# One signal for a group's value products, a power as the seed of the inverse roots, and an earlier copy of turned rows

## The chip, the cores and the metric

The kernel runs on one core of a Trainium2 chip. The metric is the device time of one execution in microseconds (us). The core has a matrix engine (TensorE, in the profile PE, with its weight loads as PEld), a vector engine (DVE), an activation engine (ACT), GpSimd (POOL) and an engine that only issues transfers (SP). Each runs its own program in its own order; they meet through semaphores.

## The reference

Four sequences of 1024 tokens, 128 channels, float32:

```
x = u + lru(layernorm(u))                 # linear recurrence, complex diagonal
z = layernorm(x)
h = z + attention(rmsnorm(z) * ln1)       # 16 heads of 8 channels, full softmax
h = h + moe(rmsnorm(h) * ln2)             # 8 experts, two per token
out = x + h

rmsnorm(v) = v * rsqrt(mean(v * v) + 1e-5)
moe: logits = v @ gate.T; the two largest are chosen and weighted by their softmax
     expert e: (silu(v @ w1[e].T) * (v @ w3[e].T)) @ w2[e].T
```

## The kernel before

The kernel has three stages. In the first (to about 245 us) the four sequences go through the recurrence and the projections to queries, keys and values. The second is attention (to about 985 us): 16 quads (a sequence and four of its heads), each with 16 groups g. In a group TensorE makes four column scores (`score_cols`, L1322), each of which ACT turns into `prob` with an exp (L853), two steps of row scores (`score_rows`, L1273) whose maxima DVE takes (L1084), and the value products of the group before (`weigh_values`, L1332): four heads, each on its own 32 columns of the array, into one bank, with two matmul instructions per head in the trace. `prob` is a ring of eight. An exp waits for its score (`col_full`) and for the value product that read its slot before (`pv_done`, set ahead by eight). After groups 7 and 15 the bank is full, ACT copies it to `oT` (`save_o`, L841), and TensorE turns it for DVE.

Behind attention, the tokens go through the routing in eight blocks of 512. Per block, ACT copies the turned attention (`turn_a`), TensorE projects it (`project`), and GpSimd does the rest: `sum_h` adds, squares and sums (L544 to L551) and makes `var` (L553); `norm_h` refines the inverse root by Newton rounds (L561 to L565) and scales the rows to `h_nrm` (L566); TensorE turns them (`turn_h`, L1356) and makes the logits; `pick_two` and `place_tokens` choose two experts per token and give each its slot, with counts from TensorE (`prefix` and `totals`, or `ranks`); `scatter` writes the rows to `by_expert_rows` with eight indirect DMAs. The seed of the root is made on DVE, with integer operations on the bits (`seed`, L1133 and L1136), between `f_mean` and `f_seed`. Blocks 0 to 5 ("early") do this during attention, in quads "even" and "odd", one block for two quads. Blocks 6 and 7 ("late") do it in the expert stage, at tiles given by the table `LATE` on TensorE and ACT and `LATE_SEED` on DVE. Before tile 0, `make_table` lists the 56 tiles of region A (blocks 0 to 5); behind block 7, it lists the 24 tiles of region B (L666 is its last operation).

The expert stage runs over 80 tiles j of 128 rows in 20 groups of four. SP loads a group of x three groups ahead (L401), TensorE turns it in tile 4g+2 (`turn_x`, L1487) and ACT copies it, scaled, to `x_T` (`save_x`, L899), in tile 4g+3. A tile is `up` (L1498) on TensorE, `gate` (L906) on ACT, the product and a copy (L1190, L1198) on DVE, a turning (L1508), `down` (L1518) two tiles later, `save_y` (L914) on ACT, and a write to `by_expert_rows` from SP (L411). Tiles 0 to 55 are region A. When all of A is written, GpSimd fetches each token's two results (`fetch`, L734, 32 tiles of tokens, two indirect DMAs each), and DVE adds them to `xacc` (`combine`, L1203 and L1206), from tile 60 on between its other work. The last eight token tiles wait for region B. The store of `out` follows.

Of the kernel before, what the change touches and what calls it, by code (L numbers as in the profile page):

```python
# [14 lines left out]
P = 128  # L15
# [47 lines left out]
def build_program(nc, x, nu2, theta2, gamma_row, b_pack, b_swap, c_re_t, c_im_t, d_t, ln1, ln2,  # L63
# [3 lines left out]
    with ctx:  # L67
        def sb(name, shape, dt=F32):
            return ctx.enter_context(nc.sbuf_tensor(name, shape, dt))

        def sem(name):
            return ctx.enter_context(nc.semaphore(name))
# [75 lines left out]
        hot = sb("hot", [P, 4, NE])  # L148
        gap = sb("gap", [P, 4])
        weigh = sb("weigh", [P, 2, 4])  # L150
        tanh = sb("tanh", [P, 4])
        slot_f = sb("slot_f", [P, 2, 4])
        slots = sb("slots", [P, 2, 4], I32)
# [43 lines left out]
        zeros, zero_out = sem("zeros"), sem("zero_out")  # L197
        gp_self = sem("gp_self")
        att_st, h_read = sem("att_st"), sem("h_read")
        f_mean, f_seed, f_norm, f_gap, f_hot, f_tanh = (  # L200
            sem(n) for n in ("f_mean", "f_seed", "f_norm", "f_gap", "f_hot", "f_tanh"))
        scattered, f_tab = sem("scattered"), sem("f_tab")
        x_loaded = [sem("x_loaded%d" % r) for r in range(3)]
        y_out = [sem("y_out%d" % r) for r in range(3)]
# [79 lines left out]
        def row_banks(pos):  # L284
            return 2 * (pos % 2)
# [7 lines left out]
        LATE = {2: ("turn_a", 6), 5: ("project", 6), 14: ("turn_h", 6), 17: ("logits", 6), 18: ("turn_a", 7),  # L293
                22: ("ranks", 6), 23: ("project", 7), 33: ("turn_h", 7), 36: ("logits", 7), 41: ("ranks", 7)}
        LATE_POS = {item: n for n, item in enumerate(LATE.values())}
        LATE_SEED = {12: 6, 31: 7}
        COMBINE = 60


# [127 lines left out]
        def _(gp):  # L427
            gp.memset(prob[:, 0, :], 0.0).then_inc(zeros, 1)
            gp.memset(ident[:, :], 0.0).then_inc(consts, 1)
            gp.memset(ones[:, :], 1.0).then_inc(consts, 1)  # L430
            gp.iota(iota_t[:, :], pattern=[[1, TILES_A]], base=0, channel_multiplier=0,
                    allow_small_or_imprecise_dtypes=True).then_inc(consts, 1)
            gp.iota(ebase[:, 0, :], pattern=[[CAP_A, NE]], base=0, channel_multiplier=0,
                    allow_small_or_imprecise_dtypes=True).then_inc(consts, 1)
            gp.iota(ebase[:, 1, :], pattern=[[CAP_B, NE]], base=ROWS_A, channel_multiplier=0,
                    allow_small_or_imprecise_dtypes=True).then_inc(consts, 1)
            gp.wait_ge(consts, 5)
            gp.affine_select(out=ident[:, :], in_=ident[:, :], compare_op=ALU.not_equal, fill=1.0,
                             base=0, pattern=[[-1, P]], channel_multiplier=1).then_inc(consts, 1)
            gp.affine_select(out=tri[:, :], in_=ones[:, :], compare_op=ALU.is_gt, fill=0.0,  # L440
# [8 lines left out]
                    r = par * ODD + CROSS  # L449
                    gp.memset(qpack[r:r + PARTS, slot, :, :, :].bitcast(F32), 0.0).then_inc(q_clear, 1)  # L450

            gp.wait_ge(consts, 9)
            for par in range(2):
                r = par * ODD + CROSS
                gp.memset(kpack[r:r + PARTS, :, :, :].bitcast(F32), 1.0).then_inc(pads, 1)
# [62 lines left out]

            four = lambda a: a.rearrange("p (t h) -> p t h", t=4)
            var, rstd, tmp = small[:, 5, 0:4], small[:, 6, 0:4], small[:, 7, 0:4]  # L520
            SUM_STEPS, NORM_STEPS, PICK_STEPS, PLACE_STEPS = 10, 12, 13, 14
            PER_FRONT = SUM_STEPS + NORM_STEPS + PICK_STEPS + PLACE_STEPS

            def fold(step, dst, src, part, op):
# [15 lines left out]
            def sum_h(t, base):  # L540

                step, count = chain(base)
                h = zres[:, bass.ds(t * 4, 4), :]
                step(gp.tensor_tensor(h, h, four(a_out), ALU.add))  # L544
                gp.sem_inc(h_read, 1)
                step(gp.tensor_tensor(xacc[:, bass.ds(t * 4, 4), :], xacc[:, bass.ds(t * 4, 4), :], h, ALU.add))
                step(gp.tensor_tensor(four(h_sq), h, h, ALU.mult))
                for n in (64, 32, 16, 8, 4, 2):
                    step(gp.tensor_tensor(four(h_sq)[:, :, 0:n], four(h_sq)[:, :, 0:n], four(h_sq)[:, :, n:2 * n],
                                          ALU.add))  # L550
                step(gp.tensor_tensor(rstd, four(h_sq)[:, :, 0], four(h_sq)[:, :, 1], ALU.add))  # L551
                gp.sem_inc(passed, 1)
                gp.tensor_scalar(var, rstd, 1.0 / H, EPS, ALU.mult, ALU.add).then_inc(f_mean, 1)  # L553
                assert count[0] == SUM_STEPS

            def norm_h(t, base):

                step, count = chain(base + SUM_STEPS)
                gp.wait_ge(f_seed, t + 1)
                for _ in range(3):  # L560
                    step(gp.tensor_tensor(tmp, rstd, rstd, ALU.mult))  # L561
                    step(gp.tensor_tensor(tmp, tmp, var, ALU.mult))
                    gp.sem_inc(passed, 1)
# [187 lines left out]
        def _(act):  # L751
# [183 lines left out]
            for j in range(TILES_T):  # L935
                gate(j)
                if j >= 2:
                    save_y(j - 2)
                if j % 4 == 3 and j + 1 < TILES_T:
                    save_x(j // 4 + 1)  # L940
                if j in LATE:
                    late_copy(*LATE[j])
                    if LATE[j][0] == "ranks":
                        shares(LATE[j][1])
# [5 lines left out]
        def _(dve):  # L950
# [175 lines left out]
                    o[:, :, 0:HD], rden[:, :].unsqueeze(2).to_broadcast([P, 4 * HQ, HD]), ALU.mult).then_inc(row_free, 1)  # L1126


            var, rstd, tmp = small[:, 5, 0:4], small[:, 6, 0:4], small[:, 7, 0:4]

            def seed(t, before):
                dve.wait_ge(f_mean, t + 1)
                dve.tensor_scalar(tmp.bitcast(I32), var.bitcast(I32), 1, None,  # L1133
                                  ALU.logical_shift_right).then_inc(dve_self, 1)
                dve.wait_ge(dve_self, before + 1)
                dve.tensor_scalar(rstd.bitcast(I32), tmp.bitcast(I32), -1.0, float(0x5F3759DF),  # L1136
                                  ALU.mult, ALU.add).then_inc(f_seed, 1)

            PER_QUAD = 6
            maxima(0, 16, 0, opening=True)  # L1140
            split_maxima(0, 16, start)
            maxima(16, PAIRS - 2, 0, opening=True)
            start += 2

            def dve_quad(i, slot, own, last=False, t=None):
                base = i * (2 * ROW_ITEMS) + slot * ROW_ITEMS
                quad = 2 * i + slot
                following = base + ROW_ITEMS
                extra = 0 if t is None else 1
                maxima(PAIRS - 2, PAIRS, base)  # L1150
                split_maxima(1, base + (pair_pos(PAIRS - 1) + 1), own)
                if not last:
                    maxima(0, 14, following)
                    finish_o(quad, 0, base + (O_OWN + 1), row_banks(O_OWN), own + 2)
                    maxima(14, 16, following)
                    split_maxima(0, following + (pair_pos(15) + 1), own + 3)
                    maxima(16, 20, following)
                    if t is not None:
                        seed(t, own + 5)
                    maxima(20, PAIRS - 2, following)  # L1160
                    finish_o(quad, 1, following + (O_LATE + 1), row_banks(O_LATE), own + (5 + extra))
                else:
                    finish_o(quad, 0, O_LAST + 1, row_banks(O_LAST), own + 2)
                    dve.wait_ge(row_free, O_LAST + 1)
                    finish_o(quad, 1, O_LAST + 2, FINAL_BANK, own + 3)

            with loop(dve, 0, 2) as i:
                own = i * (2 * PER_QUAD) + start
                dve_quad(i, 0, own)
                dve_quad(i, 1, own + PER_QUAD)  # L1170
            start += 4 * PER_QUAD
            PER_PAIR = 2 * PER_QUAD + 1
            with loop(dve, 0, EARLY - 1) as t:
                own = t * PER_PAIR + start
                dve_quad(t + 2, 0, own, t=t)
                dve_quad(t + 2, 1, own + (PER_QUAD + 1))
            start += (EARLY - 1) * PER_PAIR
            dve_quad(QUADS // 2 - 1, 0, start, t=EARLY - 1)
            start += PER_QUAD + 1
            dve_quad(QUADS // 2 - 1, 1, start, last=True)  # L1180
            start += 4

# [27 lines left out]
            for j in range(TILES_T):  # L1210
                product(j)
                if j >= 1:
                    save_ht(j - 1)
                if j in LATE_SEED:
                    seed(LATE_SEED[j], start)
                    start += 1
                if j >= COMBINE and (j - COMBINE) % 4 != 3:
                    combine(combined, start)
                    start += 1
                    combined += 1  # L1220
# [7 lines left out]
        def _(pe):  # L1228
            pe.sem_inc(pv_done, RING)

            pe.sem_inc(h_read, 1)
            pe.wait_ge(consts, 9)
            pe.wait_ge(w_in, 16 * 15)
            pe.wait_ge(b_scaled, 4)

# [90 lines left out]
            def weigh_values(g, slot, base, kind):  # L1326

                pe.wait_ge(col_free, base + (col_pos(4 * g + 3, kind) + 1))
                for head in range(HQ):
                    v = 4 * g + head  # L1330
                    kt = g % TILES
                    pe.matmul(ps[32 * head:32 * head + VW, PV_BANK, :], vpad[:, slot, kt, head, :],  # L1332
                              prob[:, v % RING, :],
                              start=(kt == 0), stop=(kt == TILES - 1), skip_group_check=True).then_inc(pv_done, 1)

            def turn_maxima(job, base, pos, kind):
                pe.wait_ge(m_split, job + 1)
# [244 lines left out]
```

## Time and profile before

| | us |
|---|---|
| median of 3 runs | 1228.52 |
| lowest, highest | 1226.97, 1229.95 |
| the profiled execution | 1228.6 |
| its span, first to last instruction | 1226.8 |
| TensorE (matmul) busy | 1005.9 (82%) |
| DVE busy | 836.2 (68%) |
| ACT busy | 666.3 (54%) |
| GpSimd busy | 418.3 (34%) |

The shares are means over stages of different kinds, so they don't say what bounds the kernel. The slices give the stages, the chain that ended last is to be read from its end, and the timelines of the engines tell at each place who waits for whom. Lines of a timeline merge consecutive instructions of one kind ("x8"), the second column is then the time from the first start to the last end, and ends of matmuls are modelled. "issue" as a releaser is time in which the engine waited for nothing that the profile shows.

### The profile page before, as it was taken

The numbers are of one execution on the slowest core, as the hardware profiler recorded it, in microseconds if no ns is written. First come the engines' busy times: TensorE is split into PE (matmuls) and PEld (weight loads), VectorE is DVE, ScalarE is ACT, GpSimd is POOL, SyncE is SP. The second block draws the span as 40 slices with busy tenths as digits, with TensorE's granted clock in tenths as the row PEclk, the third lists the DMA queues.
The fourth block names the chain that finished last, engine by engine and source line by source line (L and its number), as shares of the span: only waits on it lengthen the run. The fifth ranks groups of instructions, "written<-read, shape, count | busy, mean of one in ns | idle before, by whom it ended". The sixth has DMA issues, their size and how long they took to land. (4 is left out here: it accounts for less than half of the span.)

```text
span 1226.8 us, 21943 instructions
## 1 busy us (share of the span) xinstructions
PE 1005.9 (82%) x5592; PEld 472.9 (39%) x5592; DVE 836.2 (68%) x1286; ACT 666.3 (54%) x1382; POOL 418.3 (34%) x767
## 2 busy tenths in 40 slices
PE   0156666999999999999999999999999968777850
PEld 0034442333333344344344344434443235554530
DVE  5667658789888778888888888888884013232552
ACT  1001111577777677777777777777776534333320
POOL 6103310010110143433433523524522434644576
PEclk9978776899999989999999999999998579988985
DMA  8954566010100110100101101101100012212342
GB/s 269 383 190 137 137 172 172 1 36 10 36 26 10 37 28 10 44 25 20 43 11 33 43 10 35 43 10 35 44 1 2 17 36 64 73 50 70 96 130 71
DMA packets 61944, 81.56 MB, mean 66 GB/s; under 512 B 8512, under 2 KB 39488, under 8 KB 61504
## 3 DMA queue, kind: packets, MB, share of 16 engines
q1 hardware_dynamic: 45808, 51.93, 14.8%
q10 hardware_dynamic: 11984, 20.59, 4.6%
q0 software_dynamic: 4096, 8.40, 2.3%
q8 instruction: 24, 0.39, 0.1%
q14 instruction: 32, 0.26, 0.1%
HBM read 32.12 MB, written 48.23 MB: 65 GB/s over the span
## 5 line engine op out<-in xcount | busy, mean ns | idle before, releaser
L1084 DVE TENSOR_REDUCE smax<-ps 128x2 f32<-128x1024 f32 x512 | 601.7, 1220 | 96.7 <-PE ps L1273 93.5
L853 ACT ACTIVATE prob<-ps 128x512 f32<-128x512 f32 x1024 | 528.8, 603 | 160.2 <-PE ps L1322 157.5
L1322 PE MATMUL ps<-qpack,kpack 34*128 34x512 f32 x1024 | 383.8, 458 | 23.6 <-ACT prob L853 11.7
L1273 PE MATMUL ps<-kpack,qpack 34*128 34x512 f32 x1024 | 314.2, 452 | 10.0 <-DVE smax L1084 9.3
L1322 PEld LDWEIGHTS ps<-qpack,kpack 34*128 34x128 f32 x1024 | 172.9, 189 | 297.2 <-ACT prob L853 250.2
L1332 PE MATMUL ps<-prob,vpad 128*32 128x512 f32 x2048 | 284.7, 629 | 0.0
L1273 PEld LDWEIGHTS ps<-kpack,qpack 34*128 34x128 f32 x1024 | 138.3, 189 | 41.3 <-DVE smax L1084 28.5
L450 POOL MEMSET qpack<- 2x2048 f32 x32 | 57.6, 1799 | 207.9 <-PE ps L1322 205.2
L1190 DVE TENSOR_TENSOR prob<-ps,prob 128x256 f32<-128x256 f32 x80 | 33.9, 424 | 104.9 <-ACT prob L906 104.0
L1498 PE MATMUL ps<-w,ws 128*128 x160 | 89.1, 642 | 15.3 <-ACT ws L899 14.5
L906 ACT ACTIVATE prob<-ps 128x256 f32<-128x256 f32 x80 | 30.8, 385 | 86.3 <-PE ps L1498 86.3
L734 POOL DMA_INDIRECT vall<-by_expert_rows,slot_all x64 | 60.8, 949 | 35.7 <-issue 35.4
L634 POOL DMA_INDIRECT by_expert_rows<-qk,slots x64 | 62.5, 976 | 23.9 <-issue 17.1
L1518 PEld LDWEIGHTS ps<-w,prob 128*128 128x128 f32 x320 | 47.3, 198 | 56.1 <-issue 56.1
L1332 PEld LDWEIGHTS ps<-prob,vpad 128*32 128x32 f32 x2048 | 41.0, 109 | 66.6 <-ACT prob L853 44.8
L1518 PE MATMUL ps<-w,prob 128*128 x320 | 52.9, 289 | 10.7 <-DVE prob L1198 10.7
L544 POOL TENSOR_TENSOR zres<-zres,qk 128x512 f32 (+1 forms) x8 | 10.2, 1278 | 147.1 <-ACT qk L828 125.0
L1122 DVE RECIPROCAL rden<-ps 128x16 f32<-128x16 f32 x32 | 8.2, 257 | 59.3 <-PE ps L1385 59.3
L471 POOL TENSOR_TENSOR zres<-xacc,mv 128x1024 f32 (+1 forms) x4 | 7.6, 1903 | 115.8 <-DVE ws L1066 115.8
L1260 PE MATMUL ps<-wC,wk 128*128 128x128 f32 x128 | 26.2, 341 | 21.7 <-DVE wk L1043 21.7
L1248 PE MATMUL ps<-ws,wB 128*128 128x512 f32 x32 | 19.0, 748 | 30.3 <-ACT ws L789 30.3
L580 POOL TENSOR_TENSOR qk<-logit 128x64 f32<-128x64 f32 x32 | 8.4, 294 | 101.1 <-ACT logit L832 91.2
(211 smaller groups left out, 881.4 us busy)
## 6 DMA issues: line engine op xcount, KB each, us to landing
by_expert_rows<-prob ACTq DMA_DIRECT2D x4, 4864.0 KB, 30.9
q_parts<-qk SPq DMA_DIRECT2D x32, 256.0 KB, 3.8
k_parts<-qk SPq DMA_DIRECT2D x32, 256.0 KB, 4.0
kpack<-k_parts SPq DMA_DIRECT2D x32, 256.0 KB, 3.9
qpack<-q_parts SPq DMA_DIRECT2D x64, 128.0 KB, 3.3
vall<-by_expert_rows SPq DMA_DIRECT2D x80, 64.0 KB, 1.8
by_expert_rows<-vall SPq DMA_DIRECT2D x80, 64.0 KB
w<-w_t SPq DMA_DIRECT2D x3, 1024.0 KB, 10.1
```

Of the source, the lines that this page charges most:

```text
L450: gp.memset(qpack[r:r + PARTS, slot, :, :, :].bitcast(F32), 0.0).then_inc(q_clear, 1)
L634: gp.indirect_dma_start(by_expert_rows, bass.IndirectOffsetOnAxis(ap=slots[:, s, k:k + 1], axis=0), h_nrm[:, k * H:(k + 1) * H], None).the ...
L734: gp.indirect_dma_start(y_two[:, t % 4, s, :], None, by_expert_rows, bass.IndirectOffsetOnAxis(ap=slot_all[:, s, t:t + 1], axis=0)).then_i ...
L853: act.activation(prob[:, v % RING, :], bank(col_bank(pos, kind)), ACT.Exp).then_inc(col_free, 1)
L906: act.activation(gact[:, j % 4, :], ps[:, UP_BANK + j % 2, 0:INTER], ACT.Silu).then_inc(gate_done, 1)
L1084: dve.tensor_reduce(smax[:, half, :, pair, qt, kh], ps[:, first:first + 2, :], AX_X, ALU.max).then_inc(row_free, 1)
L1190: dve.tensor_tensor(hid[:, j % 4, :], ps[:, UP_BANK + j % 2, INTER:2 * INTER], gact[:, j % 4, :], ALU.mult).then_inc(hid_done, 1)
L1273: ins = pe.matmul(bank(first + par), qpack[r:r + ROWS, slot, half, pair, qt * P:(qt + 1) * P], kpack[r:r + ROWS, slot, pair, kh * HALF:(kh ...
L1322: pe.matmul(bank(col_bank(pos, kind)), kpack[r:r + ROWS, slot, head // 2, kt * P:(kt + 1) * P], qpack[r:r + ROWS, slot, half, head // 2, : ...
L1332: pe.matmul(ps[32 * head:32 * head + VW, PV_BANK, :], vpad[:, slot, kt, head, :], prob[:, v % RING, :], start=(kt == 0), stop=(kt == TILES ...
L1498: pe.matmul(bank(UP_BANK + j % 2), x_T[:, group % 2, k * P:(k + 1) * P], w13[:, :, bass.ds(e, 1), :].rearrange("p n a c -> p n (a c)"), st ...
L1518: ins = pe.matmul(ps[:, Y_BANK + j % 2, 0:H], hid_T[:, j % 4, c * P:(c + 1) * P], w2[:, bass.ds(e, 1), c, :].rearrange("p a h -> p (a h)") ...
```

## The change

In `weigh_values` only the last of a group's four value products signals, and it adds four. The seed of the root moves from DVE to GpSimd: `var` to the power -0.5, against a small tile `power` that holds -0.5 and is filled at the start, and two Newton rounds follow instead of three. `seed` and its two semaphores go from DVE, and its two loops over pairs of quads become one. `save_x` moves from tile 4g+3 to tile 4g+2, behind that tile's gate and result and ahead of a late copy.

```diff
+        power = sb("power", [P, 4])
...
-        LATE_SEED = {12: 6, 31: 7}
...
+            gp.memset(power[:, :], -0.5).then_inc(consts, 1)
...
-            SUM_STEPS, NORM_STEPS, PICK_STEPS, PLACE_STEPS = 10, 12, 13, 14
+            SUM_STEPS, NORM_STEPS, PICK_STEPS, PLACE_STEPS = 12, 8, 13, 14
...
-                gp.tensor_scalar(var, rstd, 1.0 / H, EPS, ALU.mult, ALU.add).then_inc(f_mean, 1)
+                step(gp.tensor_scalar(var, rstd, 1.0 / H, EPS, ALU.mult, ALU.add))
+                step(gp.tensor_tensor(rstd, var, power[:, :], ALU.pow))
...
-                gp.wait_ge(f_seed, t + 1)
-                for _ in range(3):
+                for _ in range(2):
...
-                if j % 4 == 3 and j + 1 < TILES_T:
+                if j % 4 == 2 and j + 2 < TILES_T:
                     save_x(j // 4 + 1)
...
-            def seed(t, before):
-                dve.wait_ge(f_mean, t + 1)
-                dve.tensor_scalar(tmp.bitcast(I32), var.bitcast(I32), 1, None,
-                                  ALU.logical_shift_right).then_inc(dve_self, 1)
-                dve.wait_ge(dve_self, before + 1)
-                dve.tensor_scalar(rstd.bitcast(I32), tmp.bitcast(I32), -1.0, float(0x5F3759DF),
-                                  ALU.mult, ALU.add).then_inc(f_seed, 1)
...
-                    maxima(16, 20, following)
-                    if t is not None:
-                        seed(t, own + 5)
-                    maxima(20, PAIRS - 2, following)
-                    finish_o(quad, 1, following + (O_LATE + 1), row_banks(O_LATE), own + (5 + extra))
+                    maxima(16, PAIRS - 2, following)
+                    finish_o(quad, 1, following + (O_LATE + 1), row_banks(O_LATE), own + 5)
...
-            with loop(dve, 0, 2) as i:
+            with loop(dve, 0, QUADS // 2 - 1) as i:
...
-            with loop(dve, 0, EARLY - 1) as t:
-                own = t * PER_PAIR + start
-                dve_quad(t + 2, 0, own, t=t)
-                dve_quad(t + 2, 1, own + (PER_QUAD + 1))
...
-                if j in LATE_SEED:
-                    seed(LATE_SEED[j], start)
-                    start += 1
...
-                    pe.matmul(ps[32 * head:32 * head + VW, PV_BANK, :], vpad[:, slot, kt, head, :],
-                              prob[:, v % RING, :],
-                              start=(kt == 0), stop=(kt == TILES - 1), skip_group_check=True).then_inc(pv_done, 1)
+                    ins = pe.matmul(ps[32 * head:32 * head + VW, PV_BANK, :], vpad[:, slot, kt, head, :],
+                                    prob[:, v % RING, :],
+                                    start=(kt == 0), stop=(kt == TILES - 1), skip_group_check=True)
+                ins.then_inc(pv_done, HQ)
```

## Rows read from the trace of the kernel before

**Rows 1.** The page's slices, 40 of 30.7 us: busy tenths of TensorE.

```profile
PE   0156666999999999999999999999999968777850
```

**Rows 2.** Chain that ended last: start us, us, what.

```profile
1141.34 1.07 POOL vall L734
1219.10 0.94 POOL vall L734
```

**Rows 3.** Timeline: start us, us, engine, line, operation, [idle before <- releaser].

```profile
1124.59 0.20 POOL L666 CAST qk<-qk 128x24 int32<-128x24 f32 x1
1128.68 1.11 PE L1487 MATMUL ps<-ident,vall 128*128 128x128 f32 x4 [5.61 <-DMA vall<-by_expert_rows]
```

**Rows 4.** Timeline of GpSimd, late blocks 6 and 7.

```profile
1025.48 0.20 POOL L561 TENSOR_TENSOR small<-small 128x4 f32<-128x4 f32 x1 [6.81 <-DVE small L1136]
1029.18 1.04 POOL L566 TENSOR_TENSOR qk<-zres,small 128x512 f32<-128x512 f32 x1
1066.71 1.26 POOL L544 TENSOR_TENSOR zres<-zres,qk 128x512 f32<-128x512 f32 x1 [2.70 <-DMA by_expert_rows<-qk,slots]
1073.64 0.20 POOL L553 TENSOR_SCALAR small<-small 128x4 f32<-128x4 f32 x1 [0.20 <-POOL small L551]
1078.02 1.04 POOL L566 TENSOR_TENSOR qk<-zres,small 128x512 f32<-128x512 f32 x1
```

**Rows 5.** Timelines of TensorE, then DVE, tiles 14 and 33.

```profile
1026.02 1.02 PE L1498 MATMUL ps<-w,ws 128*128 x2
1028.90 0.71 PE L1518 MATMUL ps<-w,prob 128*128 x4 [1.85 <-DVE prob L1198]
1030.37 0.63 PE L1356 MATMUL ps<-ident,qk 128*128 128x128 f32 x4
1079.21 1.09 PE L1356 MATMUL ps<-ident,qk 128*128 128x128 f32 x4 [2.49 <-POOL qk L566]
1028.33 0.42 DVE L1198 COPY prob<-ps 128x256 f32<-128x256 f32 x1 [2.02 <-issue]
1073.87 0.17 DVE L1133 TENSOR_SCALAR small<-small 128x4 int32<-128x4 int32 x1 [8.23 <-POOL small L553]
```

**Rows 6.** Timeline of TensorE: a value block, a turning, the next score.

```profile
603.38 1.06 PE L1332 MATMUL ps<-prob,vpad 128*32 128x512 f32 x8
604.38 0.66 PE L1385 MATMUL ps<-ident,oT 128*128 128x128 f32 x4
604.97 0.50 PE L1322 MATMUL ps<-qpack,kpack 34*128 34x512 f32 x1
```

**Rows 7.** Timeline of TensorE and ACT around a copy of the outputs.

```profile
548.26 1.06 PE L1332 MATMUL ps<-prob,vpad 128*32 128x512 f32 x8
549.88 2.07 ACT L853 ACTIVATE prob<-ps 128x512 f32<-128x512 f32 x4 [0.63 <-PE ps L1322]
550.96 1.07 PE L1332 MATMUL ps<-prob,vpad 128*32 128x512 f32 x8
552.17 0.60 ACT L841 ACTIVATE oT<-ps 128x512 f32<-128x512 f32 x1 [0.22 <-PE ps L1332]
552.66 2.06 ACT L853 ACTIVATE prob<-ps 128x512 f32<-128x512 f32 x4
```

**Rows 8.** Timeline of one group's end in the expert stage.

```profile
1055.27 0.60 PE L1487 MATMUL ps<-ident,vall 128*128 128x128 f32 x4
1055.70 1.02 PE L1498 MATMUL ps<-w,ws 128*128 x2
1056.76 0.38 ACT L906 ACTIVATE prob<-ps 128x256 f32<-128x256 f32 x1 [1.24 <-PE ps L1498]
1058.20 1.12 PE L1498 MATMUL ps<-w,ws 128*128 x2 [0.81 <-issue]
1059.82 0.59 PE L1498 MATMUL ps<-w,ws 128*128 x1
```

**Rows 9.** Busy time by stretch; the value behind POOL is the granted clock.

```profile
1129.00:1137.00 8.00, 7.39 (x21) 4.80 (x20) 1.50 (x4) 1.90 (x5) 0.00 (x0) 0.50 0.26 75
```

More of the change, by code:

```diff
@@ L199, in build_program @@
         att_st, h_read = sem("att_st"), sem("h_read")
-        f_mean, f_seed, f_norm, f_gap, f_hot, f_tanh = (
-            sem(n) for n in ("f_mean", "f_seed", "f_norm", "f_gap", "f_hot", "f_tanh"))
+        f_norm, f_gap, f_hot, f_tanh = (
+            sem(n) for n in ("f_norm", "f_gap", "f_hot", "f_tanh"))
         scattered, f_tab = sem("scattered"), sem("f_tab")
@@ L436, in _ @@
                     allow_small_or_imprecise_dtypes=True).then_inc(consts, 1)
-            gp.wait_ge(consts, 5)
+            gp.wait_ge(consts, 6)
             gp.affine_select(out=ident[:, :], in_=ident[:, :], compare_op=ALU.not_equal, fill=1.0,
@@ L450, in clear_maxima @@
                     gp.memset(qpack[r:r + PARTS, slot, :, :, :].bitcast(F32), 0.0).then_inc(q_clear, 1)
-            gp.wait_ge(consts, 9)
+            gp.wait_ge(consts, 10)
             for par in range(2):
@@ L1126, in finish_o @@
                     o[:, :, 0:HD], rden[:, :].unsqueeze(2).to_broadcast([P, 4 * HQ, HD]), ALU.mult).then_inc(row_free, 1)
-            var, rstd, tmp = small[:, 5, 0:4], small[:, 6, 0:4], small[:, 7, 0:4]
-            def seed(t, before):
-                dve.wait_ge(f_mean, t + 1)
-                dve.tensor_scalar(tmp.bitcast(I32), var.bitcast(I32), 1, None,
-                                  ALU.logical_shift_right).then_inc(dve_self, 1)
-                dve.wait_ge(dve_self, before + 1)
-                dve.tensor_scalar(rstd.bitcast(I32), tmp.bitcast(I32), -1.0, float(0x5F3759DF),
-                                  ALU.mult, ALU.add).then_inc(f_seed, 1)
             PER_QUAD = 6
@@ L1143, in _, with dve_quad @@
             start += 2
-            def dve_quad(i, slot, own, last=False, t=None):
+            def dve_quad(i, slot, own, last=False):
                 base = i * (2 * ROW_ITEMS) + slot * ROW_ITEMS
@@ L1148, in dve_quad @@
                 following = base + ROW_ITEMS
-                extra = 0 if t is None else 1
                 maxima(PAIRS - 2, PAIRS, base)
@@ L1170, in _ @@
                 dve_quad(i, 1, own + PER_QUAD)
-            start += 4 * PER_QUAD
-            PER_PAIR = 2 * PER_QUAD + 1
-            with loop(dve, 0, EARLY - 1) as t:
-                own = t * PER_PAIR + start
-                dve_quad(t + 2, 0, own, t=t)
-                dve_quad(t + 2, 1, own + (PER_QUAD + 1))
-            start += (EARLY - 1) * PER_PAIR
-            dve_quad(QUADS // 2 - 1, 0, start, t=EARLY - 1)
-            start += PER_QUAD + 1
+            start += (QUADS - 2) * PER_QUAD
+            dve_quad(QUADS // 2 - 1, 0, start)
+            start += PER_QUAD
             dve_quad(QUADS // 2 - 1, 1, start, last=True)
@@ L1231, in _ @@
             pe.sem_inc(h_read, 1)
-            pe.wait_ge(consts, 9)
+            pe.wait_ge(consts, 10)
             pe.wait_ge(w_in, 16 * 15)
```

## Prediction, made before the changed kernel was run

> **What bounds the kernel now.** I read the page's slices first [rows 1]: TensorE is nearly full through the attention stage, about 245 to 985 us, and has holes in the expert stage behind it. Then the chain that ended last [rows 2]: its last 80 us are GpSimd issuing 64 gathers, one every 1.25 us ((1219.10 - 1141.34) / 62), then one landing, the last sum and the store. Whatever moves the first gather moves the end by as much; what happens beside the gathers does nothing. The timelines show what releases it [rows 3]: the table of the second region is ready at 1124.79 (1124.59 + 0.20), SP loads that region's rows, TensorE, idle for 5.61 us, turns them at 1128.68, and only while it works on that region's first tiles does it finish the last two of region A; their rows are written and the gathers start. The table ends a GpSimd chain with TensorE links in it: late blocks 6 and 7 [rows 4]. From logits 6 (copied in tile 17) to the normalised rows of block 7 (1078.02 + 1.04 = 1079.06) GpSimd sets the pace; TensorE reaches their turning in tile 33 and waits for them [rows 5]. So the path to the end is: attention; tiles 0 to 17; GpSimd from logits 6 to block 7's rows; tiles 33 to 36; GpSimd to the table; tiles 54 to 57; 80 us of gathers. Tiles 18 to 32, 37 to 53 and all from 58 on hide behind GpSimd.
>
> **Part 1, signals of the values.** Three of four increments of `pv_done` go, no matmul does. Nobody waits longer for the coarser count: the exps of group g need the value products of group g-2, which TensorE issues before group g's scores, and those scores are waited for anyway. Does the array gain? A value block (eight matmuls, four signals) is followed by the next matmul 0.06 us before its modelled end (603.38 + 1.06 against 604.38), a turning with one signal 0.07 us before (604.38 + 0.66 against 604.97) [rows 6]. Equal, so the signals cost the array nothing. The waiter does gain: behind a four-signal block ACT's copy starts 0.14 us after the modelled end (550.96 + 1.07 against 552.17) [rows 7], behind a one-signal matmul 0.04 us after (1055.70 + 1.02 against 1056.76) [rows 8]. That is 0.10 us of tail for three signals, and one place waits on it: `save_o`, 32 times. There the next exp starts 1.70 us after the block's start (552.66 against 550.96), elsewhere 1.62 (549.88 against 548.26) [rows 7]: 0.08 us which TensorE's next score then waits for. 30 of these copies lie ahead of the last table: 30 x 0.08 = 2.4 us, all on the path. Bounds: 0 (if the tail belongs to the copy) and 3.
>
> The Trainium skill, page TensorE: Matmul & The Clock Gate, section The cost: per-tile semaphore tail, says that increments of tiles serialise at 26.3 ns each and that one on the last tile is enough: 79 ns for three. The 0.10 us of the rows agrees.
>
> **Part 2, the seed on GpSimd.** Removed: two DVE operations with two hand-overs, and one of three Newton rounds, 1.23 us ((1029.18 - 1025.48) / 3) [rows 4]. Added: a power over 128x4 values, p. No row shows a power. Below: the same shape costs 0.20 us in every GpSimd row [rows 4]. Above: the dearest GpSimd instruction per item is the indirect DMA, 0.94 us for 128 rows [rows 2]; 512 values at that rate are 3.8 us. I take 0.5, nearer to the rows of its own shape. The extra memset at the start runs beside the loads of x: nothing. For the six early blocks the turning stands ten groups behind the projection, 27 us at 2.70 each (550.96 - 548.26) [rows 7], and GpSimd needs 12.4 from sum to rows (1066.71 to 1079.06) [rows 4]: nothing, for p up to 10. Without its seed DVE no longer waits 8.23 us in tile 31 [rows 5], but TensorE waits for GpSimd's rows there all the same: nothing.
>
> Block 7, on the path: today 4.38 us from the start of `var` (1073.64) to that of the product (1078.02). Then a step of 0.3, p, 0.1, and 2 x 1.23: 2.86 + p = 3.36, a gain of 1.02 (1.3 at p = 0.2, a loss of 2.3 at 3.8).
>
> Block 6: `var` is there at 1018.67, the seed comes in tile 12, 6.81 us later, and the rows end at 1030.22, so TensorE can't turn them before 1030.37 in tile 14 [rows 4, 5]. Now they are ready at 1018.47 - 0.88 (part 3) + 3.36 + 1.04 = 1022.0; TensorE gets there at 1026.02 - 3 x 0.88 + 2.0 = 1025.4: no wait, for p up to 3.9. Tile 14 then takes 2.5 us (1.62, and 0.43 each for the turnings of x and h) [rows 8] instead of 4.8 (1026.02 to 1030.37, and 0.43) [rows 5]: gain 2.3. But in that tile TensorE also stood 1.85 us for a copy of DVE, which had sat 2.02 us idle with nothing that the profile shows to wait for (issue) [rows 5]. The DVE program gets shorter (two loops become one), so that hole may move or vanish; if it stays, 0.5 is gained. I take 1.5.
>
> **Part 3, the copy of turned x.** Today TensorE turns x in tile 4g+2 and ACT copies it in tile 4g+3, behind that tile's gate and result. The next group's first tile waits for it: 2.50 us from 1055.70 to 1058.20, an ordinary tile 1.62 (1058.20 to 1059.82) [rows 8]. Moved, the copy starts at the turning's end (1055.27 + 0.60) and takes about 0.7: over at 1056.6, ahead of the gate at 1056.76, which so isn't delayed. What hides it is that gap of 0.16 us; were it gone, the gate would slip by the copy's rest. Behind it stand the late copies of tiles 2, 14, 18 and 22, whose readers are two tiles or more away. So 0.88 us per group, but only on the path: tiles 4, 8, 12, 16 (3.5), tile 36 (0.88) and tile 56 (I take 0.6: the array runs at its low level there [rows 9] and fills more of the tile itself): 5.0 us. The others only make TensorE wait longer for GpSimd, before group 14 some 9.1 us (5.61 + 4 x 0.88). SP loads a group five tiles ahead of its turning: room enough.
>
> **Sum.** 2.4 + 1.0 + 1.5 + 5.0 = 9.9 us. Late next: DVE's sums (in three of four tiles from 60 on) will wait for their gathers, since a group of 6.8 us is shorter than three gathers of 2.5 us; that holds up TensorE, not GpSimd, whose gather t needs sum t-4, issued 10 us before. The profiled execution takes 1228.6 around its span of 1226.8, and the median of the three is 1228.52: 1218.6.
>
> **Rivals.** (a) The copy doesn't shorten the path: the gate slips, or it lands on a wait; 5.0 less: 1223.6. For it: only 0.16 us of room. Against: the timeline, where it fits. 12%.
>
> (b) The array is held by the signals after all: 0.10 us in each of 256 groups goes, 25.6: 1218.6 + 2.4 - 25.6 = 1195. Against it: [rows 6]. 4%. By the skill's 79 ns (same page and section) it would be 20 us, 1201.
>
> (c) The power is dear and the kernel gets slower: block 7 pays for all above 0.5 us, block 6 for all above 3.9. Even at p - 0.5 + p - 3.9 = 9.9, so p = 7.2; at p = 10 it is 1234. Against it: that is twice what the dearest row per item would make. 7%; p between 6 and 8 would be no change, 4%. The skill, page GPSIMD Engine Reference, section 2.1 Instruction dispatch, has about 6 us for the first call of freshly loaded code; it would fall into block 0, hidden, and no row shows it.
>
> (d) TensorE's clock. Behind the 5.61 us wait the granted clock was 0.50 for all of 1129 to 1137 [rows 9]. Behind a longer wait it may be back sooner (2.5 us less) or later (2 more): inside the forecast.
>
> **How the numbers follow.** Forecast 1218.6, its own range 1213.5 to 1221.5: 73%; (a) 12, (b) 4, (c) 7, no change 4. The range goes from 1213.5 (clock back sooner, tile 14 whole, p = 0.2) to 1224.5, to take in (a). 0.2%, 2.5 us, is about what a measurement can tell here: faster 0.89, same 0.04, slower 0.07.
>
> **What would show it.** Rows of the power under 1 us; `save_o` 0.04 us behind its block, its groups at 2.70 instead of 2.78; from value block to next matmul still 1.00; no wait for the copy of L899; tile 14 at 2.5 to 4.3; a longer wait before group 14; the first gather near 1131. Wrong if the power takes over 4 us, if attention shortens by more than 3 us, or if the end moves by another amount than the first gather.

## The result and the profile after

The changed kernel is slower: 1240.9 us (median of four runs, 1240.13 to 1248.43) against 1227.8 for the kernel before on the same chip (1226.97 to 1229.95), a ratio of 1.0103 with a 95% interval of 1.0059 to 1.0147. Its profiled execution took 1241.21 us around a span of 1239.4. The forecast was 1218.6. The kernel before has two usual times (of 25 runs on another chip, 12 took 1224 to 1229 us at a mean granted clock of 0.91 and 10 took 1236 to 1240 at 0.90), as much apart as the whole effect, so the argument below goes by traces, one for each run, and not by medians alone.

Read the slices first (40 of 31 us, as in [rows 1]; PEclk is TensorE's granted clock in tenths):

```profile
PE   0157666999999999999999999999999969966950
PEclk9977775999999787999998899999699559978985
```

The attention stage is still full of work, but slices 14 to 16, 22, 23 and 29 have a lower clock, where the kernel before had one such place in the stage ahead of its last quad (a fall of 13.7 us at 424.2). Three milestones divide the loss:

| | before | after | difference |
|---|---|---|---|
| first value block | 227.44 | 227.49 | 0 |
| tile 0 of the experts | 997.24 | 1021.16 | +23.9 |
| first gather, counted from tile 0 | 144.1 | 133.0 | -11.1 |
| end, counted from the first gather | 85.5 | 85.3 | -0.2 |

The second part of the kernel gained more than forecast (11.1 us from tile 0 to the first gather, against 7.5), and the gathers behind it run at their old pace, as these rows of the chain show (they answer to [rows 2]):

```profile
1154.12 1.07 POOL vall L735
1231.69 0.94 POOL vall L735
```

All of the loss lies in the attention stage. I cut it into its 16 quads (a quad is 16 groups, from value block to value block). Before, the odd quads 5 to 13 take 46.9 to 47.0 us each, all at full clock. This is the kernel before from quad 5 to 11 us into quad 15, in a view of busy time by stretch (stretch, its length, then busy us and instructions of PE, PEld, DVE, ACT, POOL; then granted clock, DMA share, GB/s):

```profile
459.90:939.50 479.60, 465.91 (x2864) 194.20 (x2863) 405.08 (x441) 365.03 (x732) 181.46 (x383) 1.00 0.09 26
```

After, these are the odd quads 5 to 13:

```profile
463.00:517.40 54.40, 53.57 (x285) 22.55 (x285) 39.72 (x43) 36.37 (x75) 22.38 (x46) 0.81 0.10 30
564.00:610.80 46.80, 45.64 (x283) 19.45 (x282) 39.68 (x43) 35.80 (x75) 21.77 (x45) 1.00 0.11 34
657.50:711.90 54.40, 53.57 (x286) 22.58 (x285) 39.78 (x43) 36.35 (x74) 22.22 (x46) 0.81 0.11 30
758.50:805.30 46.80, 45.64 (x283) 19.44 (x282) 39.71 (x43) 35.80 (x74) 21.78 (x45) 1.00 0.12 34
851.90:906.30 54.40, 53.51 (x283) 22.68 (x282) 39.79 (x43) 36.36 (x75) 22.23 (x46) 0.81 0.10 30
```

Same instructions, same busy time of DVE; only the granted clock differs, 1.00 (2.4 GHz) or a mean of 0.81, and with it 46.8 or 54.4 us. Quads 5, 9 and 13 lose their clock, 7 and 11 don't. The working:

| attention stage, after minus before | us |
|---|---|
| quads 5, 9 and 13: 7.41 + 7.46 + 7.40 | +22.3 |
| quad 4, whose clock fell in the kernel before too, for 13.7 us and now for 23.9 | +3.6 |
| the other twelve quads | -2.0 |
| sum | +23.9 |

Where does the clock fall? The two timelines show group 5 of quad 7, which keeps it, and of quad 9, which loses it:

```profile
576.03 1.07 PE L1310 MATMUL ps<-prob,vpad 128*32 128x512 f32 x8
577.03 0.28 PE L1318 MATMUL ps<-ident,mpart 128*32 128x128 f32 x1
577.15 0.96 PE L1338 MATMUL ps<-wgate,qk 128*128 128x8 f32 x8
578.04 0.50 PE L1300 MATMUL ps<-qpack,kpack 34*128 34x512 f32 x1
...
669.50 1.06 PE L1310 MATMUL ps<-prob,vpad 128*32 128x512 f32 x8
670.50 0.28 PE L1318 MATMUL ps<-ident,mpart 128*32 128x128 f32 x1
670.62 0.96 PE L1338 MATMUL ps<-wgate,qk 128*128 128x8 f32 x8
671.51 0.50 PE L1300 MATMUL ps<-qpack,kpack 34*128 34x512 f32 x1
...
673.22 1.84 PE L1310 MATMUL ps<-prob,vpad 128*32 128x512 f32 x8
```

Up to 671.51 they agree to 0.02 us. Between the value block and the next score stands the longest stretch of a quad in which TensorE has short work alone, 1.01 us (577.03 to 578.04): a turning of 128 columns and eight matmuls of 8 columns, the logits of L1338, present only in odd quads from 5 on. (Others, the counts of group 9 and the turnings of outputs and rows, take 0.6 us.) At 673.4, 2.7 us behind the first of these logits matmuls, quad 9's clock falls to 0.50, and the value block of 1.06 us takes 1.84; quad 7 goes on at 1.00. The same code, a different fate: it is not the work alone that decides. That became the question of the experiments.

The rest of the profile, by the signs that the prediction named. The copy of the outputs (as in [rows 7]) stands 0.07 us behind its block instead of 0.14, and the next exp 1.62 us behind the block's start instead of 1.70:

```profile
561.32 1.06 PE L1310 MATMUL ps<-prob,vpad 128*32 128x512 f32 x8
562.45 0.60 ACT L842 ACTIVATE oT<-ps 128x512 f32<-128x512 f32 x1
562.94 1.57 ACT L854 ACTIVATE prob<-ps 128x512 f32<-128x512 f32 x3
```

The power takes 1.05 us for 128x4 values, in all eight blocks (1.046 to 1.054), and from `var` to the product block 7 takes 3.85 us (4.38 before [rows 4]):

```profile
1089.56 0.19 POOL L554 TENSOR_SCALAR small<-small 128x4 f32<-128x4 f32 x1 [0.20 <-POOL small L552]
1089.83 1.05 POOL L555 TENSOR_TENSOR small<-small,power 128x4 f32<-128x4 f32 x1
1093.41 1.04 POOL L567 TENSOR_TENSOR qk<-zres,small 128x512 f32<-128x512 f32 x1
```

TensorE waits longer for these rows and for the x of group 14, as it must when only its own tiles got shorter (2.49 and 5.61 before [rows 3, 5]):

```profile
1094.60 1.08 PE L1335 MATMUL ps<-ident,qk 128*128 128x128 f32 x4 [10.96 <-POOL qk L567]
1144.65 1.12 PE L1466 MATMUL ps<-ident,vall 128*128 128x128 f32 x4 [10.45 <-DMA vall<-by_expert_rows]
```

### The profile page after: what moved, and what is told of

It is laid out like the page before. It is cut to its first block and busy times, and to the rows that moved or that the text cites. A ratio compares the mean times of both kernels' runs of the same rounds, so it can differ in the third digit from the quotient of the medians.

```text
span 1239.4 us, 21865 instructions
## 1 busy us (share of the span) xinstructions
PE 1031.3 (83%) x5592; PEld 482.8 (39%) x5592; DVE 832.2 (67%) x1270; ACT 669.8 (54%) x1382; POOL 417.6 (34%) x744
## 3 DMA queue, kind: packets, MB, share of 16 engines
q1 hardware_dynamic: 45808, 51.93, 14.8%
## 5 line engine op out<-in xcount | busy, mean ns | idle before, releaser
L1300 PE MATMUL ps<-qpack,kpack 34*128 34x512 f32 x1024 | 397.1, 473 | 20.2 <-ACT prob L854 7.4
L1251 PE MATMUL ps<-kpack,qpack 34*128 34x512 f32 x1024 | 326.8, 466 | 9.5 <-DVE smax L1085 8.6
L1310 PE MATMUL ps<-prob,vpad 128*32 128x512 f32 x2048 | 299.1, 659 | 0.0
L1300 PEld LDWEIGHTS ps<-qpack,kpack 34*128 34x128 f32 x1024 | 179.2, 196 | 302.1 <-ACT prob L854 242.2
L1251 PEld LDWEIGHTS ps<-kpack,qpack 34*128 34x128 f32 x1024 | 144.9, 197 | 40.5 <-DVE smax L1085 27.3
L1477 PE MATMUL ps<-w,ws 128*128 x160 | 86.1, 622 | 0.9 <-ACT ws L900 0.9
L635 POOL DMA_INDIRECT by_expert_rows<-qk,slots x64 | 62.6, 979 | 23.9 <-issue 17.1
L1497 PEld LDWEIGHTS ps<-w,prob 128*128 128x128 f32 x320 | 44.7, 193 | 54.0 <-issue 53.8
L545 POOL TENSOR_TENSOR zres<-zres,qk 128x512 f32 (+1 forms) x8 | 10.2, 1276 | 146.7 <-ACT qk L829 126.5
L907 ACT ACTIVATE prob<-ps 128x256 f32<-128x256 f32 x80 | 30.7, 384 | 52.8 <-PE ps L1477 52.5
```

Of the source, the lines that this page charges most:

```text
L635: gp.indirect_dma_start(by_expert_rows, bass.IndirectOffsetOnAxis(ap=slots[:, s, k:k + 1], axis=0), h_nrm[:, k * H:(k + 1) * H], None).the ...
L907: act.activation(gact[:, j % 4, :], ps[:, UP_BANK + j % 2, 0:INTER], ACT.Silu).then_inc(gate_done, 1)
L1251: ins = pe.matmul(bank(first + par), qpack[r:r + ROWS, slot, half, pair, qt * P:(qt + 1) * P], kpack[r:r + ROWS, slot, pair, kh * HALF:(kh ...
L1300: pe.matmul(bank(col_bank(pos, kind)), kpack[r:r + ROWS, slot, head // 2, kt * P:(kt + 1) * P], qpack[r:r + ROWS, slot, half, head // 2, : ...
L1310: ins = pe.matmul(ps[32 * head:32 * head + VW, PV_BANK, :], vpad[:, slot, kt, head, :], prob[:, v % RING, :], start=(kt == 0), stop=(kt == ...
L1477: pe.matmul(bank(UP_BANK + j % 2), x_T[:, group % 2, k * P:(k + 1) * P], w13[:, :, bass.ds(e, 1), :].rearrange("p n a c -> p n (a c)"), st ...
```

## The experiments

**First: each part alone.** Theory A: what decides is the moment at which an odd quad's short matmuls arrive, and the signals moved it. Rival B: the falls come from DVE's rewritten loop, so from the seed. All four ran on one chip, where the kernel before took 1233.8 us (median of the 25 runs).

*e1: the kernel before with one signal for a value block.*

```
-   pe.matmul(... prob[:, v % RING, :], ...).then_inc(pv_done, 1)
+   ins = pe.matmul(... prob[:, v % RING, :], ...)
+ ins.then_inc(pv_done, HQ)
```

> The kernel before with the one signal per group alone. Theory A (arrival): the changed kernel lost 24 us in attention because TensorE's granted clock fell to 0.50 behind groups 3 to 5 of quads 5, 9 and 13 (and for longer in quad 4), and it did so because the saved 0.08 us at each copy of the outputs shifts when these groups come. Then this kernel has the same falls: tile 0 at about 1021 instead of 997, the expert stage as before (144 us from tile 0 to the first gather), in all about 1252 us. Theory B (DVE): the falls come from DVE's new loop and missing seeds; then there are none here but the one of quad 4, and the kernel takes about 1226 us (2.1 less than before).

1251.1 us (1247.71 to 1251.69), ratio 1.0125 [1.0056, 1.0195]. The three falls are there, of 20.5 us each, in quads 5, 9 and 13, without any edit of DVE. Quad 4's fall lasts 23.9 us here too. So this part alone makes the loss, 21.8 us from the first value block to tile 0 (791.6 against 769.8).

*e2: the kernel before with the seed on GpSimd (all edits of the change but the signals and the place of `save_x`).*

> The kernel before with the power as seed alone (DVE without seeds and with one loop). Theory A: attention as before (tile 0 near 997, one fall of the clock, in quad 4), the expert stage 1 to 4 us shorter (block 7 gains 0.5 at a power of 1.05 us; tile 14 gains up to 2.3 if DVE's idle 2 us there is gone): 1225 to 1227 us. Theory B: attention 24 us longer, about 1250 us.

1234.7 us (1229.68 to 1242.66), ratio 1.0035 [0.9992, 1.0079]. One fall, in quad 13. From tile 0 to the first gather 140.8 us, 3.3 less than before. The 1225 to 1227 expected didn't come: the fall in quad 13 wasn't in it.

*e3: the kernel before with the earlier copy of turned x.*

```
-   if j % 4 == 3 and j + 1 < TILES_T:
+   if j % 4 == 2 and j + 2 < TILES_T:
        save_x(j // 4 + 1)
```

> The kernel before with the earlier copy of turned x alone. Both theories: attention as before. The copy is worth 0.9 to 1.0 us per group on tiles 4, 8, 12, 36 and 56 (tile 14 waits for block 6 here, tile 16 counts): 5 us, about 1223 us. If the expert stage's 11 us came mainly from elsewhere (the hole of DVE, the clock before region B), less than 3 us.

1223.1 us (1215.28 to 1263.98), ratio 0.9913 [0.9863, 0.9962]: faster than the kernel before. Tile 0 to first gather 132.8 us, 11.3 less than before. Like the kernel before, it keeps its full clock from quad 5 until 11 us into quad 15:

```profile
459.90:939.50 479.60, 465.93 (x2864) 194.21 (x2863) 405.06 (x441) 364.90 (x731) 181.03 (x383) 1.00 0.09 26
```

*e4: the changed kernel with four signals again.*

> The changed kernel with its four signals per group back, so the seed and the copy of x without the signals. Theory A: attention as before (tile 0 near 997, one fall of the clock) and the expert stage of the changed kernel (133 us from tile 0 to the first gather): 11 us less than before, about 1217 us. Theory B: attention as in the changed kernel, about 1243 us.

1227.6 us (1217.18 to 1233.68), ratio 0.9949 [0.9902, 0.9995]. One fall, in quad 13; tile 0 to first gather 133.4 us:

```profile
462.00:850.00 388.00, 377.49 (x2321) 158.63 (x2321) 327.76 (x350) 294.69 (x592) 149.83 (x299) 1.00 0.09 28
850.70:871.20 20.50, 20.50 (x82) 8.42 (x82) 10.76 (x10) 10.66 (x22) 9.03 (x31) 0.50 0.04 13
```

e4 has DVE's new loop and only one of the three falls, e1 has the old loop and all three: so rival B doesn't explain the three falls. It isn't out for quad 13, which e2 and e4 lose and e3 keeps; f3, below, shows that the old loop loses that quad too.

**Second: the arrival moved by itself.** Eight kernels (f1 to f4, g1 and g2 for this, g3 and g4 for the third question) ran on two chips on which everything was disturbed: the kernel before itself took 1355 to 1368 us there (medians), the 64 gathers 96 to 101 us instead of 79, and TensorE waited up to 3.5 us in groups 11 to 13 of odd quads and lost its clock there as well. For what it waited isn't shown. Their times decide nothing. Two of their expectations stand for the eight:

> The kernel before with warming matmuls of 3.07 us more, chosen so that its quads 5, 9 and 13 come as those of the changed kernel do against the clock's changes in both traces. Theory A: falls in those quads, 2 or 3 of 7.4 us, 1245 to 1254 us. Theory D: none, 1231 us.

> The kernel before with a shorter last warming matmul (300 instead of 512 columns), so that everything behind it stands some 0.35 us sooner. Theory A: the odd quads 5, 9 and 13 now arrive where those of the changed kernel did; three falls of 20.5 us, attention 769.8 + 22 = 792 us, the whole about 1250 without any part of the change. Rival D: no additional fall, 769.8 us, the whole as the kernel before.

1415.8 us and 1413.9 us (ratio 1.0434 [1.0346, 1.0522] for the second). Both lost the clock for 181 us, from 1.4 us ahead of the first value block, which no other kernel did; so their times and their number of falls can't be compared with the expected ones. The other six gave 1334.8 (f1), 1348.3 (f2), 1352.7 (f3, the kernel before 0.85 us later, ratio 0.9878 [0.9726, 1.0030]), 1356.1 (g1), 1363.2 (g3) and 1344.1 us (g4); f1 and g1 were run again as h1, f2 as h2, g3 as k1 and g4 as h3.

The traces of the moved kernels before show one thing all the same. Apart from the falls in groups 11 to 13, they have falls 2.6 to 3.3 us behind the first logits matmul, as in the changed kernel: f3 in quads 7, 11 and 13, f4 in quad 5, g2 in quads 5 and 13. Quad 7 of f3 (the kernel before, one warming matmul more):

```profile
594.65 0.96 PE L1359 MATMUL ps<-wgate,qk 128*128 128x8 f32 x8
...
597.25 1.87 PE L1332 MATMUL ps<-prob,vpad 128*32 128x512 f32 x8
```

```profile
597.40:617.90 20.50, 20.50 (x82) 8.43 (x78) 10.76 (x11) 10.61 (x22) 9.19 (x31) 0.50 0.04 13
```

So these falls need neither the one signal nor DVE's new loop.

*h1: the changed kernel, all 0.43 us later.*

```
            for _ in range(4):
                pe.matmul(bank(PV_BANK), ident[:, :], flat13[:, 0:HALF], start=True, stop=True)
+           pe.matmul(ps[:, PV_BANK, 0:256], ident[:, :], flat13[:, 0:256], start=True, stop=True)
```

> The changed kernel with one more matmul of 256 columns ahead of the first attention group: all behind it 0.43 us later. Theory A (arrival): quads 5, 9 and 13 start as late after the clock's rise as in the kernel before; no fall in them; first value block to tile 0 about 771 us, the whole about 1219. Rival D (the changed program as such): three falls of 20.5 us as before, 793 us, the whole about 1241.

1223.0 us (1218.97 to 1248.56) against 1238.2 for the kernel before on that chip, ratio 0.9879 [0.9804, 0.9954]. Quads 5, 9 and 13 keep their clock, as expected, but quads 7 and 11 lose it, which I had not expected. Nor did the quads arrive as planned: quad 4's own fall lasted 10.2 us instead of 23.9, so quad 5 comes 4.7 us sooner after the clock's rise than in the changed kernel, not 0.43 later. The odd quads of h1, as shown above for the changed kernel:

```profile
457.70:504.50 46.80, 45.63 (x283) 19.42 (x282) 39.71 (x43) 35.81 (x75) 21.45 (x45) 1.00 0.12 35
551.10:605.50 54.40, 53.53 (x283) 22.52 (x282) 39.72 (x43) 36.35 (x75) 22.27 (x46) 0.81 0.11 30
652.10:698.90 46.80, 45.62 (x283) 19.43 (x282) 39.70 (x43) 35.81 (x75) 21.77 (x45) 1.00 0.12 34
745.60:800.00 54.40, 53.51 (x287) 22.61 (x287) 39.76 (x43) 36.36 (x74) 22.28 (x46) 0.81 0.10 30
846.60:893.40 46.80, 45.59 (x287) 19.41 (x288) 39.70 (x43) 35.81 (x74) 21.84 (x45) 1.00 0.12 34
```

Five copies of one loop body: a shift of the start, with no other edit, changes which of them lose the clock. Rival D of the expectation (the program as such) falls.

*h2: the changed kernel, 0.85 us later (one full warming matmul more).*

> The changed kernel with one more matmul of 512 columns ahead of the first group: all behind it 0.85 us later. Theory A: no fall in quads 5, 9 and 13, but perhaps in 7 and 11, which now arrive where no odd quad of any run has stood; the whole between 1219 and 1234. Rival D: three falls in 5, 9 and 13 as before, 1241.

1247.5 us (1214.03 to 1247.98). The profiled execution lost its clock in quads 5, 9 and 13 again, and in 14; the run of 1214.0 us, 33 us faster, has no trace, but it can hardly have held the same falls, so one program need not have one pattern in all its executions. At first sight that is rival D; the table below shows that these quads didn't arrive later at all: the clock fall of quad 4 was 3.4 us shorter than in the changed kernel (20.5 against 23.9), quad 4 itself 1.0 us, and that took the shift away.

*k3: the changed kernel again, on another chip.*

> The changed kernel once more, beside the other two. By theory A its quads are where they were, so the falls of 20.5 us come again in quads 5, 9 and 13: 1241. If they are a matter of the chip or of chance, one of them at least is missing in the profile, and the whole stands near 1220 to 1233.

1239.5 us (1236.56 to 1247.04) against 1229.4, ratio 1.0069 [1.0017, 1.0120]. The same three falls:

```profile
480.00:500.50 20.50, 20.50 (x83) 8.41 (x82) 10.79 (x10) 10.70 (x22) 8.91 (x29) 0.50 0.04 13
674.60:695.10 20.50, 20.50 (x82) 8.52 (x76) 10.81 (x11) 10.55 (x22) 9.08 (x31) 0.50 0.04 13
869.10:889.60 20.50, 20.50 (x82) 8.61 (x76) 10.88 (x11) 10.54 (x22) 9.07 (x31) 0.50 0.04 13
```

From the traces, the start of each odd quad in us after TensorE's clock rose at the head of the attention stage (at 221.1 to 224.0 us); bold: it lost its clock.

| profiled execution | 5 | 7 | 9 | 11 | 13 |
|---|---|---|---|---|---|
| before | 237.1 | 331.0 | 424.8 | 518.5 | 612.4 |
| e3 | 237.2 | 331.0 | 424.8 | 518.7 | 612.5 |
| e4 | 237.2 | 330.9 | 424.7 | 518.5 | **612.3** |
| e2 | 237.1 | 330.9 | 424.6 | 518.3 | **612.0** |
| h1 | 235.5 | **328.9** | 429.9 | **523.4** | 624.4 |
| after | **240.2** | 341.2 | **434.7** | 535.7 | **629.1** |
| k3 | **240.2** | 341.2 | **434.6** | 535.7 | **629.2** |
| e1 | **240.1** | 341.3 | **434.8** | 535.8 | **629.3** |
| h2 | **240.0** | 341.1 | **434.5** | 535.5 | **628.9** |

The table is what settles the point. Four executions, of three programs and on at least three chips, arrive alike to 0.4 us and share the fate of every quad; before and e3 share theirs, and e2 and e4, with the same TensorE code in that quad, arrive 0.1 to 0.5 us sooner in quad 13 and lose the clock there. In all falls in quads 5 to 13 of the table the clock goes 2.6 to 3.1 us behind the first logits matmul. In the loop of the kernel before two quads take 93.8 us, with one signal 93.5: the signals' own gain moves every later arrival. The larger move comes by way of quad 4. The signals' gain brings that quad 0.6 us sooner (405.49 against 406.00, from a first value block 0.05 later); its fall then begins 3.4 us sooner and lasts 10.2 longer, and quad 5 arrives 3.1 us later (240.2 against 237.1). Why quad 4's fall grows isn't shown.

**Third: is it the short matmuls?**

*k1: the changed kernel with the logits one group sooner (group 4), away from the turning of the maxima.*

```
-   "odd": {3: ("turn_h",), TURN: ("m_own", "logits"), ...
+   "odd": {3: ("turn_h",), 4: ("logits",), TURN: ("m_own",), ...
```

> The changed kernel with the logits of the odd quads in group 4 instead of group 5, where the turning of the maxima stands; the same instructions. If the clock falls because logits and turning of the maxima together thin out one stretch: no fall in an odd quad, attention about 771 us, the whole 1216 to 1219. If the eight short logits matmuls alone are enough: falls in some of the odd quads, at other quads than 5, 9 and 13 since they come 2.7 us sooner, 1226 to 1241.

1287.4 us (1228.23 to 1305.34). Of quads 7 to 13 one lost its clock, quad 13, and it fell 12.9 us behind the quad's start; in the falls of after, e1, e2, e4, h1, h2 and k3 that is 15.8 to 16.2 us. The fall moved with the logits, 3 us where they had moved by one group of 2.7. Quad 5, which came while quad 4's fall still lasted, got its clock back at 485.0 and lost it at 488.4, 1.1 us behind its first logits matmul, for 27.3 us. The fall in quad 13 lasted three times as long as that:

```profile
874.10:956.00 81.90, 81.90 (x318) 33.87 (x319) 46.11 (x48) 42.57 (x84) 22.15 (x46) 0.50 0.07 20
```

It is no cure. The 61 to 65 us that the clock of quad 4 stayed low here, in k2 and in h3 (10.2 to 23.9 in the others) I can't explain; nothing of quad 4 was edited.

*h3: one full matmul (512 columns, 0.85 us) ahead of the logits. k2: half of one (256 columns).*

```
    elif name == "logits":
+       pe.matmul(out, ident[:, :], flat13[:, 0:HALF], start=True, stop=True)
        for k in range(4):
```

> The changed kernel with one full matmul (512 columns of float32, 0.85 us, its result overwritten) ahead of the logits of each odd quad. If the stretch of eight short matmuls is what lets the clock fall, the three falls are gone at the price of 6 x 0.85 = 5.1 us: attention about 776 us, the whole about 1224. If that stretch has nothing to do with it: 799 us and 1246.

> The changed kernel with one matmul of 256 columns (0.43 us) ahead of the logits of each odd quad, half of the filler that took the falls away. If half is enough: no fall in quads 7 to 13, at 6 x 0.43 = 2.6 us: 1221. If not: two or three falls of 7.5 us each: 1236 to 1244.

h3: 1237.7 us (1215.73 to 1246.81); none of quads 7 to 13 lost its clock, and each took 0.7 us more than in the kernel before, as the filler costs (quads 7 and 9 of h3):

```profile
572.50:620.20 47.70, 46.53 (x285) 19.83 (x284) 39.74 (x43) 35.85 (x75) 21.78 (x45) 1.00 0.12 34
666.80:714.50 47.70, 46.52 (x285) 19.83 (x284) 39.71 (x43) 35.83 (x75) 21.74 (x45) 1.00 0.12 34
```

Quad 4's long fall ate the gain (13.5 us), so the 1224 expected didn't come in the profiled execution; the best run, 1215.7, has no trace. k2: 1231.7 us (1224.79 to 1235.78), ratio 0.9990 [0.9938, 1.0042]; one fall, in quad 7, 16.5 us into the quad. Four quads at full clock behind a full filler agree with the idea that the short matmuls let the clock go, and so does g4, with no fall behind the logits of quads 5 to 13, but these quads also arrived at other times; that the filler cures is not shown. Short matmuls aren't needed for every fall either: in the kernel before the clock also falls in quad 4, 2.0 us behind a wait of 2.40 us, and 11 us into quad 15, ahead of that quad's logits, and in h2 in quad 14.

## Why the prediction was wrong

**The step that failed** is in part 1: "Three of four increments go, no matmul does", and then 30 x 0.08 = 2.4 us, "all on the path", with nothing in the sum for TensorE's clock in the attention stage. The term itself was right: the twelve quads without a change of clock are 2.0 us shorter, 0.17 each, against 0.16 by the prediction (two copies of 0.08). What was missing is that a shift of this size, added up over a long stage, moves all later work against a clock that the kernel doesn't set. In the kernel before the clock of the odd quads 5 to 13 never fell, so I took the attention stage as a fixed 770 us and looked for the clock only behind waits, as rival (d), in the expert stage. The trace of before held a warning that I read past: a fall of 13.7 us in quad 4, at 424.2, with no wait over 2.4 us before it. The result is 22.3 us of three falls and 3.6 of quad 4's longer one; without them the changed kernel would stand near 1215 (an estimate: 1240.9 - 25.9).

**Rivals.** None of the four was it. (a) is refuted by e3, where the earlier copy alone shortens the path. (b), the array held by signals, is refuted: value block to next matmul stays 1.00 us (576.03 to 577.03). So is (c): the power costs 1.05 us, twice what I took, far from the 7 that would turn the sign.

**The tail of signals.** The Trainium skill, page TensorE: Matmul & The Clock Gate, section The cost: per-tile semaphore tail, gives 26.3 ns for each increment; the trace agrees: three fewer bring the copy's start 0.07 us nearer to the block (0.14 to 0.07) and its group from 2.78 to 2.70 us. About the first call, the Trainium skill, page GPSIMD Engine Reference, section 2.1 Instruction dispatch, has some 6 us for freshly loaded code; the first power here (448.6) starts 0.3 us after `var` (448.3) and takes as long as the others, so no row here shows it.

**The seed.** Block 7 by the prediction 2.86 + p; with the measured p that is 3.91, the trace has 3.85: gain 0.5 instead of 1.0. Tile 14 went from 4.81 to 2.48 us, gain 2.3: DVE's idle 2.02 us of "issue" is gone with the new program (it is there in e1 and e3, 1.93 us in e3, and gone in e2 and e4). Alone, in e2, the seed brought 3.3 us to the first gather; I had 2.5.

**The copy of x.** I had 5.0 us; alone, in e3, it brought 11.3. The room of 0.16 us was enough: a group of four tiles with nothing between them takes 6.71 us instead of 7.70 (tiles 8 to 11), so 1.0 instead of 0.88. The rest I had called hidden. From tile 0 to the first gather, in us, from start to start:

| stretch | before | e3 | e4 | after |
|---|---|---|---|---|
| tile 0 to block 6's logits on GpSimd | 41.6 | 37.4 | 35.5 | 35.2 |
| to block 7's normalised rows | 39.2 | 37.1 | 36.5 | 37.1 |
| to block 7's logits on GpSimd | 10.9 | 9.6 | 10.0 | 10.7 |
| to the table of the second region | 35.7 | 34.6 | 36.5 | 36.3 |
| to the first gather | 16.8 | 14.0 | 14.8 | 13.7 |
| sum | 144.1 | 132.8 | 133.4 | 133.0 |

Rows two and four are the ones I took as GpSimd's own pace. They aren't quite: inside them GpSimd waits for ACT's tanh and for its scattered rows, and both waits shrink when the tiles are shorter. Block 6, before and then e3:

```profile
1048.63 0.19 POOL L610 TENSOR_SCALAR weigh<-tanh 128x4 f32<-128x4 f32 x1 [1.23 <-ACT tanh L845]
```

```profile
1043.53 0.20 POOL L610 TENSOR_SCALAR weigh<-tanh 128x4 f32<-128x4 f32 x1 [0.47 <-ACT tanh L845]
1060.38 1.26 POOL L544 TENSOR_TENSOR zres<-zres,qk 128x512 f32<-128x512 f32 x1 [1.47 <-DMA by_expert_rows<-qk,slots]
```

(the second wait was 2.70 us before [rows 4]). The last row of the table, where I took 0.6, gave 2.8 in e3 and 3.1 after: as the longer wait ahead of group 14 begins sooner, so does the low clock behind it, and it is over 3.1 us after the turning at 1144.65 instead of 8 us or more in the kernel before [rows 3, 9]. That is rival (d)'s "back sooner", which I had inside the range with 2.5 us. How much of it is the copy's is open: in e1, with the old copy, the last row is 2.3 us shorter than before as well (14.5, with a low clock of 3.4 us there instead of 10.2), and the whole stretch 1.0 (143.1), with no edit in it. So much it can move without an edit of its own. In the changed kernel's stretch of low clock TensorE was busy for 3.15 of 10.2 us only:

```profile
1137.60:1147.80 10.20, 3.15 (x9) 2.12 (x10) 0.00 (x0) 0.98 (x2) 2.40 (x10) 0.50 0.21 61
```

**Both together** bring 10.7 (e4) to 11.5 us (k3), and 12.1 to 13.5 in h1, h2, h3, k1 and k2, where the clock stood otherwise around tile 0; not 3.3 + 11.3. In e4 the table comes no sooner than in e3 (118.6 us after tile 0 against 118.8), though block 7's rows are 2.5 us earlier: part of it goes into a wait for the last scattered rows, 3.20 us in e4 and 3.00 after, 1.35 in e3:

```profile
1106.90 0.20 POOL L647 TENSOR_TENSOR counts<-run,ebase 128x8 f32<-128x8 f32 x1 [1.35 <-DMA by_expert_rows<-qk,slots]
```

```profile
1131.45 0.21 POOL L648 TENSOR_TENSOR counts<-run,ebase 128x8 f32<-128x8 f32 x1 [3.00 <-DMA by_expert_rows<-qk,slots]
```

Why these rows land later stays open: from the last scatter's issue to the wait's end it is 2.3 us in seven of the undisturbed profiles and 3.0 to 4.2 in five, all five with the seed and the earlier copy, but three kernels with both have 2.3.

**What beats the kernel before**: e3, the earlier copy alone (0.9913, and its attention arrives as the kernel before's), and by less e4 (0.9949). h1, the whole change with 0.43 us of warming more, has 0.9879 [0.9804, 0.9954], but two falls of its own, and five of the seven runs that it is compared with took 1237 to 1239 us.

## What to carry to other kernels

A saving in a loop that keeps TensorE full is not safe by its own cost alone (in this kernel 2.0 us saved came with 25.9 lost): before counting it, look for stretches of short matmuls in the loop body and for falls of the clock that are there already, and afterwards compare the granted clock iteration by iteration, not its mean. Where some iterations of one body take longer than others with the same instructions, change the alignment (a warming matmul more) as an experiment, before blaming the edit. And work that "hides behind" another engine's chain has to be checked for waits inside that chain.

## What was not expected of the hardware

- Behind the same 1 us of short matmuls TensorE's clock fell to 0.50 for 20.5 us or didn't fall at all, depending on the arrival: 240.0 to 240.2 us after the clock's rise it fell in four of four profiled executions, at 341.1 to 341.3 in none of four. One fall costs the quad 7.4 us. What the chip goes by, I can't say.
- Arrivals repeat to 0.4 us over 400 us and between chips in the profiled executions, so that the pattern of falls can look like a property of the edit. It needn't hold for all executions of a program (h2: three runs near 1247.5 us, one of 1214.0).
- A power of 128x4 float32 values on GpSimd takes 1.05 us, five times the 0.20 us of a multiplication of that shape.
